# One masked normalisation per half, reordered queues, and the last 128 tokens in two halves of 128 columns

## What is computed

```python
h = patches @ W.T + b + pos_emb                       # 512 x 768 by 768 x 256
h = h + attention(layernorm(h))                       # 16 heads, S = 16 tokens an image
def bitlinear(x, w):
    scale = clip(mean(abs(w), axis=1), 1e-5, None)
    return x @ (clip(round(w / scale), -1, 1) * scale).T
z = layernorm(h)
r = relu(bitlinear(z, w_fc) + gate * (z @ v.T @ fast_b.T @ u.T))
h = h + bitlinear(r * r, w_proj)                      # hidden 1024
```

## Time and profile before

| | |
|---|---|
| median of 3 runs | 70.86 us (68.31 to 72.33) |
| profiled execution | 68.79 us |
| its span, first to last instruction | 67.0 us |
| TensorE busy | 59.1 us (88%) |
| VectorE busy | 44.2 us (66%) |
| ScalarE busy | 38.8 us (58%) |
| GpSimd busy | 27.7 us (41%) |

### The profile page before, as it was taken

The page is one execution under the profiler, slowest core; times in us unless marked ns, Lnnn a source line. Parts: engine busy times, 40 slices in busy tenths (PEclk is TensorE's granted clock), DMA queues, the critical chain, the costliest instruction groups (busy, mean ns, idle before and its releaser), DMA issues.

```text
span 67.0 us, 2165 instructions
## 1 busy us (share of the span) xinstructions
PE 59.1 (88%) x894; PEld 53.3 (80%) x894; DVE 44.2 (66%) x96; ACT 38.8 (58%) x78; POOL 27.7 (41%) x44
## 2 busy tenths in 40 slices
PE   5949999999989999999957969999989999999900
PEld 5918888889968999798936856988969899999800
DVE  0000019657999996999799992723866599989670
ACT  2602001834195969973799699828799358873000
POOL 6500016398788659999956200003900000000700
PEclk9999999999999999999999999999999999999999
DMA  0899999999810000000000000000000000000053
GB/s 1 226 298 296 372 405 404 397 334 370 330 67 0 0 10 0 0 10 0 10 0 0 10 5 5 0 0 10 0 0 0 0 0 0 0 0 0 10 189 124
DMA packets 3371, 6.50 MB, mean 97 GB/s; under 512 B 385, under 2 KB 1314, under 8 KB 3362
## 3 DMA queue, kind: packets, MB, share of 16 engines
q1 hardware_dynamic: 3344, 6.35, 27.1%
q10 hardware_dynamic: 18, 0.03, 0.2%
HBM read 5.85 MB, written 0.52 MB: 95 GB/s over the span
## 4 chain that ended last, share of the span: by engine, by line
PE 57%; DVE 19%; ACT 11%; DMA 5%; issue 4%
PE psum L308 12%; PE psum L497 11%; PE psum L468 9%; DMA pos_sb<-pos 5%; PE psum L374 5%; PE psum L348 5%; PE psum L314 3%; DVE z L792 3%; PE psum L403 3%; PE psum L477 2%; PE psum L328 2%; DVE prob_n L855 2%; DVE bn L784 2%; DVE prob_t L862 2%; PE psum L454 2%
## 5 line engine op out<-in xcount | busy, mean ns | idle before, releaser
L733 ACT ACTIVATE head_sb<-psum,fc_scale 128x256 f32<-128x256 f32 x16 | 6.6, 470 | 3.3 <-PE psum L477 2.7
L497 PE MATMUL psum<-mlp_t,sq_hi 128*128 128x256 f32 x32 | 7.8, 283 | 0.0
L605 ACT ACTIVATE std<-mv,eps_sb 128x1 f32<-128x1 f32 x8 | 2.2, 289 | 9.5 <-DVE mv L786 9.5
L497 PE MATMUL psum<-mlp_t,sq_lo 128*128 128x256 f32 x32 | 7.7, 280 | 0.0
L782 DVE TENSOR_TENSOR h<-psum,posb 128x256 f32<-128x256 f32 x4 | 1.6, 412 | 8.9 <-PE psum L308 8.9
L1072 POOL TENSOR_TENSOR tail_sb<-tail_sb,h 128x256 f32<-128x256 f32 x2 | 1.4, 736 | 13.7 <-DVE tail_sb L891 13.7
L468 PE MATMUL psum<-zt_hi,fc_t 128*128 128x256 f32 x32 | 6.8, 283 | 0.0
L468 PE MATMUL psum<-zt_lo,fc_t 128*128 128x256 f32 x32 | 6.6, 278 | 0.0
L497 PEld LDWEIGHTS psum<-mlp_t,sq_hi 128*128 128x128 f32 x32 | 6.0, 189 | 0.0
L497 PEld LDWEIGHTS psum<-mlp_t,sq_lo 128*128 128x128 f32 x32 | 6.0, 189 | 0.0
L308 PE MATMUL psum<-head_sb,tail_sb 128*128 128x256 f32 x24 | 5.5, 379 | 0.0
(11 more groups left out here) (114 smaller groups left out, 165.6 us busy)
## 6 DMA issues: line engine op xcount, KB each, us to landing
head_sb<-head SPq DMA_DIRECT2D x6, 256.0 KB, 4.7
fc_sb<-w_fc SPq DMA_DIRECT2D x2, 512.0 KB, 6.7
mlp_sb<-w_mlp SPq DMA_DIRECT2D x2, 512.0 KB, 9.3
tail_sb<-tail SPq DMA_DIRECT2D x2, 384.0 KB, 6.1
out<-tail_sb SPq DMA_DIRECT2D x4, 128.0 KB, 1.7
kqv_sb<-w_k SPq DMA_DIRECT2D x1, 256.0 KB, 6.1
kqv_sb<-w_q SPq DMA_DIRECT2D x1, 256.0 KB, 6.1
kqv_sb<-w_v SPq DMA_DIRECT2D x1, 256.0 KB, 5.5
```

The source lines that it names most:

```text
L497: mm = pe.matmul(mlp_ps[f * BH + b], part[:, n % RING, a, b * P:(b + 1) * P], mlp_t[:, 2 * j + a, :], start=j == 0 and a == 0 and i == 0 a ...
L605: nc.scalar.activation(std[:, which, b:b + 1], mv[:, which, b, 1:2], ACT.Sqrt, bias=eps_sb[:, 0:1]).then_inc(std_ready, 1)
L733: nc.scalar.activation(relu[:, n % PART_RING, a, :], FCB[n][:, a * HT:(a + 1) * HT], ACT.Relu, scale=fc_scale[:, 0, m:m + 1]).then_inc(rel ...
```

## The change

1. The position rows' DMA goes from ScalarE's queue to SP's, behind the fourth piece of `head_sb`, and their product goes behind the first eight embedding products.
2. The four key spreads of the first half: ScalarE does two, VectorE none. The second half's key copy goes from ScalarE to VectorE. `zt_low(1)` goes behind the sums of fc, and GpSimd's `residual(1)` behind the rounding of the second weight matrix.
3. `softmax_divide` becomes one instruction of 1024 elements a partition, which multiplies by `srec_two`, a small table of 1/sum times the mask.
4. `turn_mlp(1)` goes from before the first hidden products to behind `project(1)`. Banks 1 and 2 of PSUM change places in `z2t_ps`, `low_ps` and `FCB`.
5. ScalarE copies `z2t_hi[0]` before `duo_rows(1)`; `mlp_signs(1)` goes behind the stds of the second half and before `squares(1)`, and the copy of `z2t_hi[1]` before `relus(3)`.
6. In the second half, `mlp_out` treats the last block of 128 tokens as two halves of 128 columns, each with its own PSUM bank.
7. VectorE scales and adds these halves one by one; SP issues the output of the first and ScalarE that of the second.
8. Block 2's sum goes to GpSimd.

```diff
-        z2t_ps = [bank[2], bank[3]]
-        low_ps = [bank[2][:, 0:HT], bank[4][:, 0:HT]]
-        FCB = [bank[i] for i in (0, 1, 2, 0, 5, 1, 2, 0)]
-        mlp_ps = [bank[7][:, 0:E], bank[7][:, E:2 * E], bank[3][:, 0:E], bank[6][:, 0:E]]
+        z2t_ps = [bank[1], bank[3]]
+        low_ps = [bank[1][:, 0:HT], bank[4][:, 0:HT]]
+        FCB = [bank[i] for i in (0, 2, 1, 0, 5, 1, 2, 0)]
+        mlp_ps = [bank[7][:, 0:E], bank[7][:, E:2 * E], bank[3][:, 0:E]]
+        end_ps = [bank[6][:, 0:P], bank[4][:, 0:P]]
...
                 sp.dma_start(head_sb[:, k, :], head[:, k, :]).then_inc(head_in[k], 16)
+                if k == POS_FETCH:
+                    sp.dma_start(pos_sb[:, :], pos).then_inc(pos_in, 16)
...
-            for b in range(BLOCKS):
-                if b < BH:
-                    sp.wait_ge(out_pool, b + 1)
-                else:
-                    sp.wait_ge(out_dve, b - BH + 1)
+            for b in range(BLOCKS - 1):
+                sp.wait_ge(out_pool, b + 1)
                 sp.dma_start(out[b * P:(b + 1) * P, :], out_sb[:, b, :]).then_inc(out_done, 16)
-            sp.wait_ge(out_done, 16 * BLOCKS)
+            sp.wait_ge(end_ready, 1)
+            sp.dma_start(out[(BLOCKS - 1) * P:, 0:P], out_sb[:, BLOCKS - 1, 0:P]).then_inc(out_done, 16)
+            sp.wait_ge(out_done, 16 * (BLOCKS + 1))
...
+                if f == 0:
+                    whole = [(a, b) for b in range(BH) for a in range(2)] if last else \
+                        [(a, b) for a in range(2) for b in range(BH)]
+                else:
+                    whole = [(a, 0) for a in range(2)]
+                for a, b in whole:
...
+                if f == 1:
+                    for h in range(2):
+                        for a in range(2):
+                            for i, part in enumerate((sq_hi, sq_lo)):
+                                mm = pe.matmul(end_ps[h], part[:, n % RING, a, P:2 * P],
+                                               mlp_t[:, 2 * j + a, h * P:(h + 1) * P],
+                                               start=j == 0 and a == 0 and i == 0, stop=last and a == 1 and i == 1)
+                        if last and h == 0:
+                            mm.then_inc(end_tile, 1)
...
-            pe.wait_ge(pos_in, 16)
-            pe.matmul(pos_ps, pos_sb[:, 0:P], pos_sb[:, P:P + E], start=True, stop=True).then_inc(pos_done, 1)
             for k in range(LAST):
                 pe.wait_ge(head_in[k], 16)
                 for b in range(BH):
                     embed(k, b)
+            pe.wait_ge(pos_in, 16)
+            pe.matmul(pos_ps, pos_sb[:, 0:P], pos_sb[:, P:P + E], start=True, stop=True).then_inc(pos_done, 1)
...
-            key_spread(0, (0,))
+            key_spread(0, (0, 3))
...
+            norm_std(1, 1, var2, std2)
             mlp_signs(0)
-            norm_std(1, 1, var2, std2)
+            copy_out(z2t_hi[0][:, :, :], z2t_ps[0][:, :], z2t_turned, 1, z2t_hi_ready)
             duo_rows(1)
-            copy_out(z2t_hi[0][:, :, :], z2t_ps[0][:, :], z2t_turned, 1, z2t_hi_ready)
-            mlp_signs(1)
-            copy_out(scale_row[:, :], row_ps, row_done, 1, row_copied)
...
             low_high(0)
+            copy_out(scale_row[:, :], row_ps, row_done, 1, row_copied)
             relus(0)
             squares(0)
             relus(1)
-            squares(1)
             norm_std(2, 1, var2, std2)
             norm_std(3, 1, var2, std2)
+            mlp_signs(1)
+            squares(1)
             relus(2)
+            copy_out(z2t_hi[1][:, :, :], z2t_ps[1][:, :], z2t_turned, 2, z2t_hi_ready)
             relus(3)
-            copy_out(z2t_hi[1][:, :, :], z2t_ps[1][:, :], z2t_turned, 2, z2t_hi_ready)
...
+            act.wait_ge(end_ready, 2)
+            act.dma_start(out[(BLOCKS - 1) * P:, P:E], out_sb[:, BLOCKS - 1, P:E]).then_inc(out_done, 16)
...
-            def softmax_divide(f, i):
+            def softmax_divide(f):
                 dve.wait_ge(recip_ready, f + 1)
+                dve.tensor_tensor(srec_two[:, f, :, :], srec[:, f, :].rearrange("p (n o) -> p n o", o=1).broadcast_to(
+                    [P, SCORES, 2]), img_mask.rearrange("p (o i) -> p o i", o=1).broadcast_to([P, SCORES, 2]),
+                    ALU.mult).then_inc(recip_two_ready, 1)
+                dve.wait_ge(recip_two_ready, f + 1)
                 if f > 0:
                     dve.wait_ge(pt_ready, BH * f)
-                dve.scalar_tensor_tensor(prob_n[:, :, i, :], prob[:, f, :, :], img_mask[:, i:i + 1],
-                                         per_row(srec, f), ALU.mult, ALU.mult).then_inc(norm_ready, 1)
-
-            def softmax_turn(f):
-                dve.wait_ge(norm_ready, 2 * f + 2)
+                dve.tensor_tensor(
+                    prob_n[:, :, :, :],
+                    prob[:, f, :, :].rearrange("p n (o s) -> p n o s", o=1).broadcast_to([P, SCORES, 2, S]),
+                    srec_two[:, f, :, :].rearrange("p n (i o) -> p n i o", o=1).broadcast_to([P, SCORES, 2, S]),
+                    ALU.mult).then_inc(norm_ready, 1)
...
+            def end_result(h):
+                c = slice(h * P, (h + 1) * P)
+                if h == 0:
+                    dve.wait_ge(end_tile, 1)
                 else:
                     dve.wait_ge(mlp_step, 2 * STEPS)
...
+                dve.tensor_tensor(out_sb[:, BLOCKS - 1, c], end_ps[h], scale_row[:, c], ALU.mult).then_inc(end_scaled, 1)
+                dve.wait_ge(end_scaled, h + 1)
+                dve.tensor_tensor(out_sb[:, BLOCKS - 1, c], out_sb[:, BLOCKS - 1, c], h2[:, BLOCKS - 1, c],
+                                  ALU.add).then_inc(end_ready, 1)
```

More of the change, by code:

```diff
@@ L144, in build_program @@
         srec = sb("srec", [P, HALVES, SCORES])
+        srec_two = sb("srec_two", [P, HALVES, SCORES, 2])
         y_duo = sb("y_duo", [P, 2, GRP, BH, PPB, PAIR])
@@ L492, in mlp_out @@
                 last = j == STEPS - 1
-                order = [(a, b) for b in range(BH) for a in range(2)] if last else \
-                    [(a, b) for a in range(2) for b in range(BH)]
-                for a, b in order:
+                if f == 0:
[4 more added lines that the diff above has]
+                for a, b in whole:
                     for i, part in enumerate((sq_hi, sq_lo)):
@@ L558, in _ @@
             values(1)
+            turn(0, z, z2t_ps[0], z2_ready, z2t_turned)
             pe.wait_ge(mlpt_ready, 1)
-            turn(0, z, z2t_ps[0], z2_ready, z2t_turned)
             spread_scale()
-            pe.wait_ge(duo_ready, 6)
-            turn_mlp(1)
             hidden_main(0, 0, (z2t_hi,))
@@ L570, in _ @@
             project(1)
+            turn_mlp(1)
             hidden_low(0, 1)
@@ L642, in query_copy @@
                 last.then_inc(q_copied, 1)
-            def key_copy(f):
-                act.wait_ge(k_done, f + 1)
-                for g in range(GRP):
-                    last = nc.scalar.activation(k_sb[:, f, g, :], k_ps[f][:, g * HT:(g + 1) * HT],
-                                                ACT.Identity, bias=k_bias[:, g:g + 1])
-                last.then_inc(k_copied, 1)
             def key_spread(f, heads):
@@ L824, in key_copy, with key_spread @@
                                   ALU.add).then_inc(k_copied, 1)
-            def key_spread(f, heads):
-                dve.wait_ge(k_copied, f + 1)
-                src = k_sb[:, f, :, :].rearrange("p g (n s) -> p (g n) s", s=S)
-                for h in heads:
-                    last = dve.tensor_scalar(k_spread[:, f, :, h, :], src, quad_mask[:, h:h + 1], None, ALU.mult)
-                last.then_inc(k_spread_dve, 1)
-            def per_row(t, f):
-                return t[:, f, :].rearrange("p (n o) -> p n o", o=1).broadcast_to([P, SCORES, S])
+            def key_spread():
+                dve.wait_ge(k_copied, 2)
+                src = k_sb[:, 1, :, :].rearrange("p g (n s) -> p (g n) s", s=S)
+                dve.tensor_scalar(k_spread[:, 1, :, 3, :], src, quad_mask[:, 3:4], None,
+                                  ALU.mult).then_inc(k_spread_dve, 1)
             def softmax_shift(f):
@@ L923, in _ @@
             normalise1(3)
-            key_spread(0, (3,))
             fc_sums(0)
-            zt_low(1)
             fc_sums(1)
@@ L929, in _ @@
             low_rank_factors()
+            zt_low(1)
             softmax_shift(0)
-            key_spread(1, (3,))
+            key_copy(1)
+            key_spread()
             softmax_sum(0)
-            softmax_divide(0, 0)
-            softmax_divide(0, 1)
-            softmax_turn(0)
+            softmax_divide(0)
+            softmax_turn(0, 0)
+            softmax_turn(0, 1)
             softmax_shift(1)
@@ L967, in _ @@
             scale_result(1)
-            for b in (2, 3):
-                scale_result(b)
-                add_result(b)
+            scale_result(2)
+            end_result(0)
+            end_result(1)
         @block.gpsimd
@@ L1074, in _ @@
             key_spread(0, (1, 2))
```

(5 more changed lines are left out.)

36 lines of the change are left out of this document (19 added, 17 removed).

## The result

The changed kernel takes **73.84 us** (median of 4 executions, 72.11 to 74.72), the kernel before, run beside it, 69.69 us (68.31 to 72.33). The ratio is **1.057 (95% interval 1.049 to 1.065)**: slower. It leaves out executions over 1.5% above the fastest of their kernel. The profiled execution takes 73.08 us with a span of 71.3, against 68.79 and 67.0: +4.3, where I had summed +2.75.

The account below looks back on a forecast made before the run. TensorE's streams, and VectorE and ScalarE in the middle, were taken to bound the kernel. Terms 0.1 + 0 + 1.0 + 0.4 + 1.75 - 0.5 = +2.75 on a median of 70.86 gave 73.6 us, range 70.9 to 76.5.

Parts of the forecast that it names:

- Narrow products: Second half's last four steps: a 128-column product costs what a 256-column one does, 0.114 us; +1.75 us (0 to +5.3).
- The other two cases: Narrow products as cheap as their columns, costing nothing (0.12), or as dear as full f32 ones, +5.3 us (0.19).
- One normalisation a half: Second half's softmax: one pass of 1024 saves nothing alone, but GpSimd's late residual delays VectorE; +1.0 us (-0.55 to +1.0).
- the residual blocks: Second half's normalisation: GpSimd's two-source residual holds up VectorE, +1.0 us; the rival, residual out of the way, had 0.24.
- TensorE's `project(0)` follows `yt`: After the second softmax: project's first tile is there at 38.45, when VectorE is free, so only the transposes' end counts.
- The clock: Whole kernel: granted clock at its upper level, 2.4 GHz, in all 40 slices, so it enters no term.
- Network's queues: Second normalisation to the second half's copy: copy 0.62 later, first hidden product 0.2 sooner; +0.4 us (0 to +0.7).
- The wait was there: Before the second half's first hidden product: TensorE idles 0.55 us for the late copy of z2t_hi[1].
- First half: First half's softmax and key copies: second exponentials begin at 31.8 as before; 0 us (-0.2 to +0.3).
- Position rows: Front: position rows on SP's queue gain nothing and cost slightly; TensorE starts on patches at about 4.6; +0.1 us (0 to +0.4).
- The end: Behind the last product: halved output lets VectorE finish 0.5 us sooner; -0.5 us (-0.6 to -0.2).
- the exclusion that I had just priced: VectorE passes with two SBUF inputs and GpSimd instructions exclude each other; priced at +1.0 us in the second half's normalisation.

Follow-up runs that it names:

- e10: The kernel before with only the narrow end added (last 128 tokens' products and output in two halves): 72.18 us.
- e1: The changed kernel with GpSimd's residual(1) early again, right behind residual(0): 71.91 us.
- e5: The changed kernel with the normalisation in two passes of 512 again, residual(1) left late: 72.88 us, 1.040 of before.
- e6: The changed kernel with two passes of 512 again and residual(1) early again: 71.75 us, 1.029 of before.
- e3: The changed kernel with 28 unread products of ones on TensorE between fold_v and project(0), filling its wait for yt: 72.97 us.
- e12: The kernel before with only the network's new queues (turn_mlp(1), mlp_signs, z2t_hi copies, banks): 71.37 us.
- e2: The changed kernel with 256-column products for the last tile again; only scale, sum and DMA in halves: 72.14 us.
- e4: The changed kernel with the position rows' DMA back on ScalarE's queue and their product first on TensorE: 74.44 us.
- e7: The changed kernel with only the network's queues (turn_mlp(1), mlp_signs, z2t_hi copies, banks) as before: 74.19 us.
- e11: The kernel before with only the merged normalisation pass of 1024 elements, all queues as before: 71.98 us.
- e9: The changed kernel with 256-column products, two passes of 512 and residual(1) early again: 69.39 us.
- e8: The changed kernel with residual(1) early again and 28 unread products filling TensorE's wait before project(0): 71.79 us, 1.042 of before.

## Why the prediction was right, and where it was not

Slower, 73.6 forecast and 73.84 measured. That closeness is partly luck: the median of before beside it was 69.69 and not 70.86, and the profiled difference is +4.3 where I had +2.75.

- **Narrow products**, +1.75: right. +1.71 in the changed kernel, +1.66 alone (e10), pace 0.112 for 0.114. 16 columns, 128 and 256 come 0.11 to 0.118 apart, so up to 256 the columns don't set the pace; that the load does is inferred from its being the same in all three. The other two cases are out. The Trainium skill's (TensorE: Matmul & The Clock Gate, Back-to-back issue gap) 81 ns for 128 columns doesn't hold for these 4-byte operands: 112 ns.
- **One normalisation a half**, +1.0: the end of the transposes is as reckoned (+1.01 from the shift; the residual blocks, 0.98 in e1, 1.07 in e5). By the rule of the Trainium skill (SBUF — State Buffer, Who interferes with whom) this had to be, and these runs agree (2.21 against 1.23 in e1, 1.75 against 0.68 in e5 and e6); the trace of before had no such meeting. But the step "TensorE's `project(0)` follows `yt`: its first tile is there at 38.45, when VectorE is free" failed. It took `project` as hidden because its first tile is. The merged pass puts `yt` behind 1024 elements instead of 512, and the second tile, the second mean and the turning come later: up to 0.6.
- **The clock** "enters no term": this is the step that failed most. I read the level off a profile without that wait. The wait of 2.2 us, which followed from my own times (`yt` at 37.3, `fold_v` done at 35), brought the lower level for some 3.4 us: at least 0.85 in the changed kernel, 0.71 in e1; filled, it brought none (e3). With the merged pass's part the two cost 1.45, and no term of mine had either.
- **Network's queues**, +0.4: +0.2 alone (e12), inside its range. The wait was there (0.39, foreseen 0.55), and the gain ahead of it was 0.30 and not 0.2.
- **First half**, 0: -0.15; the first softmax's sum starts 0.28 sooner (16.38 against 16.66 behind the first sum of `h`), and what sped it up was not taken apart. **Position rows**, +0.1: +0.40 in this execution, with 0.43 of waiting for one piece of rows; not a fixed cost. TensorE started on the patches at 3.71 and not at 4.6, and my 0.211 a product divides 5.07 by 24 where 24 records have 23 distances: 0.220.
- **The end**, -0.5: -0.2. I had GpSimd take tile 2's sum and didn't apply to it the exclusion that I had just priced: VectorE's 0.29 beside GpSimd's 0.72 became 0.65.

## What to carry to other kernels

Splitting a matmul's columns in two saves nothing where products of fewer columns come no faster; look for rows of the same type with fewer columns (here 16, 128 and 256 all at 0.11 to 0.118 us), and split only what comes behind. When two passes become one, ask what stood between them: here a small sum that fed TensorE cost more by going behind the larger pass than the pass saved. When an instruction is moved away from a collision, look at what it meets in its new place, and at what else was moved there. And where a change lets TensorE stand still for more than a microsecond in the middle of a stream, price the same products at the lower clock as a case of its own.

## What the runs showed of the hardware

**The clock falls in some executions and not in others.** Mean granted clock by execution: with a wait of 2.2 us (changed, e2, e4) it is 0.94 to 0.98 in all twelve; with 2.0 (e7) in five of six; with 1.52 (e1) 0.96 and 0.98 in two of four and 1.00 in two; with 1.43 (e5) 0.97 and 0.98 in four of six; with 1.23 (e11) 0.97 in two of six and 1.00 in four; with 0.45 (e9) and 0.35 (e6) 0.98 in one of six each; with the wait filled (e3, e8) it is 0.99 or 1.00 in all ten. The waits are those of the profiled executions; a mean of 0.99 can come from the time behind the last product alone, as in e12's profile. So a single profile doesn't tell what such a wait costs.

**The front runs at the lower level for longer in some executions, and the row of the granted clock doesn't show it.** TensorE's timeline in e12, its weight loads for the first products (ns min/median/max, starts), and those of `project(0)` in e11, which lies in a stretch with a granted clock of 0.50:

```profile
4.53 1.22 PE L509 MATMUL psum<-pos_sb 17*128 17x256 f32 x2 [1.04 <-DMA pos_sb<-pos]
...
L308 PEld LDWEIGHTS psum<-head_sb x24: 190/335/337, 5.7 to 13.4; 128*128 128x128 f32 x24
...
L405 PEld LDWEIGHTS psum<-proj_sb,yt x8: 186/190/338, 38.9 to 40.6; 128*128 128x128 f32 x8
```

A load of this type takes 190 ns at the upper level and 338 at the lower one (e11). In e12's front it takes 335 to 337, though the row says 1.00 there; so that 1.00 is no reading of the upper level. Slice by slice of 1 us the loads' mean falls from 337 to 190 in the slice from 11 us in e12, from 9 in e11, from 8 in e10, from 7 in e3, from 6 in e5 and from 5 in e8, and the first sums come at 13.26, 12.18, 11.58, 11.41, 10.78 and 10.14; in the kernel before they are at 190 from the first product (5.06) on, and its first sum comes at 9.76. The same 24 products take 8.3 us in e12, 7.13 in e11, 6.90 in e10 and 5.45 in before, the position product 1.22 and not 0.69. So the clock bears on the front too, where my prediction took the row's 9 for a reading.

What decides how long it lasts isn't shown. The waits before the position product (0.79 in e10, 1.15 in e11, 1.04 in e12; 0.95 in before, 0.64 in e4, both quick) don't order it. With the position rows behind the patches TensorE waits only 0.2 to 0.6 us after its warming products, and seven of nine profiled first sums lie at 9.48 to 10.16 (the others 10.78 and 11.41), against two of five with the rows ahead. Fitting that, five of e9's six executions are below 70 us and one of eleven of the kernel before beside it; but of all 33 of the kernel before eight are, and four of them among the eleven beside e5 to e8. That the shorter wait is the cause is only argued: no run changed the wait alone.
